# Quantised FFN: two places by turns for rows and scales, product clamped in bfloat16, first tile's second smoothing on VectorE, the gate's tanh later

## Chip, cores and metric

One core of one Trainium2 chip runs the whole program. The metric is device time in microseconds (us) of one execution; lower is better.

## What is computed

Two blocks of a gated cross-attention network, each an attention and a feed-forward part, on x of 8 x 256 rows of 1024 numbers. The diff touches only the last part, the quantised feed-forward network of the second block. For each row:

```
xs    = bf16(layernorm(x)) * inv_smooth          # once with inv_gate, once with inv_up
scale = max(max|xs| / 127, 1e-8)                 # one number per row
q     = clip(round(xs / scale), -127, 127)
gate  = (qg @ w_gate.T) * sg * s_wgate           # 1024 -> 512
up    = (qu @ w_up.T)   * su * s_wup
inter = bf16(clip(silu(gate) * up, -10, 10))
qi, si = quantise(inter * inv_inter)             # as above
out   = (qi @ w_down.T) * si * s_wdown           # 512 -> 1024
x     = x + tanh(g_ffn[1]) * out
```

## The kernel before

The parts before it (lag attention, routed experts, context attention) are not touched. `quantised_ffn` handles the 2048 rows as 16 tiles of 128 rows; a tile lies on the 128 partitions. Each engine has its own instruction list, written out by hand, and they meet through semaphores. `pipeline` calls an engine's `step` once for every tile number t from -3 to 17; within it, `on(2)` is the tile t + 2, `on(0)` the tile t, and so on, so that four stages of four tiles are worked on in one step. The steps 3 to 12 are a hardware loop (ten turns), the others are written out.

The stages of one tile, by engine:

- ACT normalises the rows to bfloat16 (`xf`), last in its step, for tile t + 3.
- POOL multiplies by the two smoothing rows (`xs_g`, `xs_u`), for tile t + 2.
- DVE takes the largest absolute value of each (`peak`), makes the scale (`scale_x`) and its reciprocal (`inv_x`).
- ACT rounds by adding a large constant (`xq_g`, `xq_u`), for tile t + 1; PE transposes; ACT subtracts the constant (`q`).
- PE multiplies by the gate and up weights into banks 4 and 5, for tile t; DVE scales them (`gated`, `up`), ACT takes silu, DVE multiplies (`hidden`) and clamps to bfloat16 (`hidden_b`), POOL smooths (`hs`), DVE makes `scale_h` and `inv_h`.
- ACT rounds (`hq`), PE transposes and multiplies by the down weights for tile t - 1; DVE scales (`y`) and POOL adds the residual (`final`) for tile t - 2; SP stores it.

DVE's order in a step is `y`, `gated`, `up`, product, clamp, two peaks, `scale_x`, `inv_x`, the peak of `hs`, `scale_h`, `inv_h`. POOL's is `xs_g`, `xs_u`, `final`, `hs`. ACT's is `xq_g`, `xq_u`, `hq`, silu, `q_h`, four times `q`, `xf`.

`xf`, `xs`, `inv_x` and `y` have one place each. POOL's `xs` of a tile therefore waits for ACT's reading of the tile before (semaphore `magic_x`). `ffn.rows` (shown as `ffn_row` in the trace) are the smoothing rows; `norm` makes mean and scale of the rows, and for the last batch (tiles 14 and 15) this is done within this part: `norm.variance` on DVE, `norm.on_pool` on POOL.

Of the kernel before, what the change touches and what calls it, by code (L numbers as in the profile page):

```python
# [1613 lines left out]
def quantised_ffn(nc, ffn, w_down_T, s_gate, s_up, s_down, inv_inter, gate, X, norm, out):  # L1614
# [4 lines left out]
    with ExitStack() as ctx:  # L1619
# [18 lines left out]
        plus_magic = sb("plus_magic", [P, 1])  # L1638
        xf = sb("xf", [P, D], BF16)
        xs = [sb("xs_g", [P, D]), sb("xs_u", [P, D])]  # L1640
        xq = [sb("xq_g", [P, D]), sb("xq_u", [P, D])]
        q = [sb("q_g", [P, KD, P], BF16), sb("q_u", [P, KD, P], BF16)]
        peak, inv_x = (sb(n, [P, 2]) for n in ("peak", "inv_x"))
        scale_x = sb("scale_x", [P, TILES, 2])
        gated, up = (sb(n, [P, HIDDEN]) for n in ("gated", "up"))
        hidden_b = sb("hidden_b", [P, HIDDEN], BF16)
        hs = sb("hs", [P, HIDDEN])
# [14 lines left out]
        def pipeline(eng, step):  # L1662

            def one(t):
                step(lambda off: t + off if not isinstance(t, int) or 0 <= t + off < TILES else None)
            for t in range(-3, 3):
                one(t)
            with eng.Fori(3, TILES - 3) as t:  # L1670
# [24 lines left out]
        def _(pool):  # L1695
# [5 lines left out]
                               pattern=[[-1, P]], channel_multiplier=1).then_inc(s["consts"], 1)  # L1701
            pool.dma_start(w_d[:].rearrange("p (k n) -> p k n", k=KH), w_down_T.rearrange("(k p) n -> p k n", p=P)).then_inc(s["w_d_in"], 16)
            norm.prepare(pool)
            for i in range(2):
                pool.wait_ge(ffn.rows_in[i], 16)

            def step(on):
                a, m, e = on(2), on(0), on(-2)
                if isinstance(a, int) and a == 2:
                    norm.on_pool(pool, B - 1, 0)  # L1710
                if a is not None:
                    for i, ready in enumerate(("xg_ready", "xu_ready")):
                        pool.wait_ge(s["xf_ready"], a + 1)

                        at_least(pool, s["magic_x"], 2 * (a - 1) + i + 1 if not (isinstance(a, int) and a == 0) else 0)
                        pool.tensor_tensor(xs[i][:], xf[:], smooth[i][:], ALU.mult).then_inc(s[ready], 1)  # L1716
                if e is not None:
                    pool.wait_ge(s["y_ready"], 2 * e + 2)
                    at_least(pool, s["stored"], 16 * e)
                    pool.tensor_tensor(final[:], y[:], tile_of(X, e), ALU.add).then_inc(s["added"], 1)  # L1720
                if m is not None:
                    if isinstance(m, int) and m == 0:
                        pool.wait_ge(vec_in[4], 16)
                    pool.wait_ge(s["hidden_b"], m + 1)
                    at_least(pool, s["magic_h"], m)
                    pool.tensor_tensor(hs[:], hidden_b[:], smooth_h[:], ALU.mult).then_inc(s["hs"], 1)  # L1726
# [3 lines left out]
        def _(act):  # L1730
            act.wait_ge(s["gate_in"], 16)
            act.activation(tg[:], tg[:], ACT.Tanh).then_inc(s["tg_done"], 1)
            act.wait_ge(s["consts"], 3)

            def step(on):
                a, f, m, d = on(3), on(1), on(0), on(-1)
                if f is not None:
                    for i in range(2):
                        act.wait_ge(s["scale_ready"], f + 1)
                        at_least(act, s[("turned_g", "turned_u")[i]], f)  # L1740
                        act.activation(xq[i][:], xs[i][:], ACT.Identity, scale=inv_x[:, i:i + 1], bias=plus_magic[:, 0:1]).then_inc(s["magic_x"], 1)  # L1741
                if d is not None:
# [17 lines left out]
                if a is not None:  # L1760
                    at_least(act, s["xg_ready"], a)
                    at_least(act, s["xu_ready"], a)
                    if not isinstance(a, int) or a >= TILES - 2:
                        act.wait_ge(norm.ready, 1)
                    act.activation(xf[:], tile_of(X, a), ACT.Identity,
                                   scale=norm.scale[:, bass.ds(a, 1)], bias=norm.shift[:, bass.ds(a, 1)]).then_inc(s["xf_ready"], 1)
            pipeline(act, step)

        @block.vector
        def _(dve):  # L1770
            norm.variance(dve, X, B - 1, 0)

            def step(on):
                a, m, e = on(2), on(0), on(-2)
                if isinstance(m, int) and m == 0:
                    dve.wait_ge(vec_in[2], 16)
                    dve.wait_ge(vec_in[3], 16)
# [5 lines left out]
                if e is not None:  # L1783
                    for i in range(2):
                        dve.wait_ge(s["down_pe"], 2 * e + i + 1)
                        at_least(dve, s["added"], e)
                        dve.scalar_tensor_tensor(out=y[:, i * 512:(i + 1) * 512], in0=bank[7 - i][:], scalar=scale_h[:, bass.ds(e, 1)],  # L1787
                                                 in1=scale_d[:, i * 512:(i + 1) * 512], op0=ALU.mult, op1=ALU.mult).then_inc(s["y_ready"], 1)
# [4 lines left out]
                if m is not None:  # L1793
# [4 lines left out]
                    dve.wait_ge(s["up"], m + 1)  # L1798
                    dve.tensor_tensor(bank[5][:], bank[4][:], up[:], ALU.mult).then_inc(s["hidden"], 1)  # L1799
                    dve.wait_ge(s["hidden"], m + 1)  # L1800
                    at_least(dve, s["hs"], m)
                    dve.tensor_scalar(hidden_b[:], bank[5][:], SWIGLU_LIMIT, -SWIGLU_LIMIT, ALU.min, ALU.max).then_inc(s["hidden_b"], 1)  # L1802
                if a is not None:
                    for i, ready in enumerate(("xg_ready", "xu_ready")):
                        dve.wait_ge(s[ready], a + 1)
                        dve.tensor_reduce(peak[:, i:i + 1], xs[i][:], AX_X, ALU.max, apply_absolute_value=True).then_inc(s["chain"], 1)  # L1806
                    dve.wait_ge(s["chain"], 3 * a + 2)
# [16 lines left out]
        def _(pe):  # L1824
            pe.wait_ge(s["consts"], 3)

            def step(on):
# [116 lines left out]
```

## Time and profile before

| | |
|---|---|
| median of 3 runs | 1379.06 us (1376.68 to 1380.38) |
| the profiled execution | 1376.35 us, its span 1374.6 us |
| the quantised part | from 1201.4 us of the span to its end |
| one turn of its loop | from 1283.25 to 1292.61 us, as an example |
| granted clock of PE, mean over the span | 0.974 of full speed |

The page counts busy time over the whole span, which has stages of quite different kinds. For a change in one stage the timeline of that stage is to be read, engine by engine: a row of it has the start, the length, the instruction, and in brackets how long the engine stood idle before it and what ended that. The length of an instruction can hold a wait that no semaphore shows.

### The profile page before, as it was taken

To read this page: it belongs to the slowest core of one execution; us is meant where nothing else is said; L and a number is where in the kernel's file an instruction comes from. 1 tells how busy PE (TensorE), PEld (TensorE's weight loads), DVE (VectorE), ACT (ScalarE), POOL (GpSimd) and SP (SyncE) were. 2 spreads that over 40 slices of the span, in tenths; PEclk is the share of its full clock that TensorE was granted. 3 is DMA by queue.
4 is the path that set the end of the run, shared out by engine and by line. 5 is a ranking of instruction groups with operands and counts; after the bars stand their busy time and mean duration, and the time that the engine had idled before them with its cause. 6 is when DMAs were issued, how large, how long until landed. Compare 5 with 4: busy or idle time off the path is not lost. (4 is left out here: it accounts for less than half of the span.)

```text
span 1374.6 us, 20874 instructions
## 1 busy us (share of the span) xinstructions
PE 1259.7 (92%) x6498; PEld 857.0 (62%) x6498; DVE 779.1 (57%) x2009; ACT 501.8 (37%) x875; POOL 579.4 (42%) x964
## 2 busy tenths in 40 slices
PE   4899999999977999999999998999999999858786
PEld 2354544545433955448887787888888898535443
DVE  3878888888774572005533333444454443368895
ACT  2544444444432600013322222232222322178884
POOL 5676867768653000003222221523212231168885
PEclk9999999999998999999999999999999999979999
DMA  5210211402001800416777874526334331121111
GB/s 198 89 66 31 92 61 45 184 15 88 35 0 47 324 1 7 144 59 243 256 250 249 275 260 158 191 85 134 107 110 123 94 103 50 62 69 46 61 61 77
DMA packets 52481, 156.38 MB, mean 114 GB/s; under 512 B 5952, under 2 KB 16192, under 8 KB 52288
## 3 DMA queue, kind: packets, MB, share of 16 engines
q1 hardware_dynamic: 39152, 113.60, 23.2%
q0 software_dynamic: 13264, 41.95, 10.7%
q8 instruction: 37, 0.61, 0.2%
q14 instruction: 28, 0.23, 0.1%
HBM read 113.06 MB, written 45.61 MB: 115 GB/s over the span
## 5 line engine op out<-in xcount | busy, mean ns | idle before, releaser
L1213 PEld LDWEIGHTS ex_bank<-ex_xT,ex_gu 128*112 128x112 f32 x1248 | 140.5, 177 | 24.9 <-issue 23.9
L1213 PE MATMUL ex_bank<-ex_xT,ex_gu 128*112 128x128 f32 x1248 | 143.6, 273 | 2.7 <-issue 1.8
L44 PE MATMUL xa_bank<-fT_high,M_hi 128*128 128x256 f32 x512 | 143.9, 281 | 0.0
L46 PE MATMUL xa_bank<-fT_high,M_lo 128*128 128x256 f32 x512 | 142.9, 279 | 0.0
L45 PE MATMUL xa_bank<-fT_low,M_hi 128*128 128x256 f32 x512 | 142.9, 279 | 0.0
L52 PE MATMUL la_bank<-la_osum,la_tab 128*128 128x512 f32 x256 | 120.6, 616 | 13.1 <-POOL la_osum L295 11.9
L295 POOL TENSOR_TENSOR la_osum<-la_oprod 128x512 f32<-128x512 f32 x64 | 80.2, 1273 | 96.1 <-DVE la_oprod L481 96.1
L1077 POOL TENSOR_TENSOR ex_small<-listed,ex_small 128x1 int32<-128x1 int32 x42 | 15.4, 368 | 225.0 <-DVE Wk L1155 224.9
L44 PEld LDWEIGHTS xa_bank<-fT_high,M_hi 128*128 128x128 f32 x512 | 96.5, 189 | 0.3
L46 PEld LDWEIGHTS xa_bank<-fT_high,M_lo 128*128 128x128 f32 x512 | 96.6, 189 | 0.0
L45 PEld LDWEIGHTS xa_bank<-fT_low,M_hi 128*128 128x128 f32 x512 | 96.3, 188 | 0.0
L52 PEld LDWEIGHTS la_bank<-la_osum,la_tab 128*128 128x128 f32 x256 | 47.7, 196 | 75.2 <-issue 48.3
L1433 DVE SCALAR_TENSOR_TENSOR X<-ffn_row,weights,X 128x1024 f32<-128x1024 f32 x30 | 38.6, 1285 | 92.3 <-DMA ffn_row<-produced,xa_small_u 91.8
L52 PE MATMUL la_bank<-la_v_raw,la_tab 128*128 128x512 f32 x128 | 64.4, 627 | 24.4 <-ACT la_v_spec L351 13.8
L52 PE MATMUL la_bank<-la_wT,la_tab 128*128 128x512 f32 x192 | 85.1, 593 | 1.2 <-ACT la_wT L378 1.2
L481 DVE TENSOR_TENSOR la_oprod<-la_bank,la_v_spec 128x512 f32<-128x512 f32 x128 | 79.7, 684 | 9.0 <-POOL la_osum L295 4.6
L1364 ACT ACTIVATE xa_G<-xa_bank,shift 128x256 f32<-128x256 f32 x64 | 30.4, 475 | 126.1 <-PE xa_bank L46 125.6
L1223 PE MATMUL ex_bank<-ex_dn,ex_hT 112*128 112x512 f32 x156 | 73.5, 593 | 0.4 <-DVE ex_hT L1166 0.4
L1155 DVE COPY Wk<-ex_xr 128x1024 f32 (+1 forms) x41 | 28.0, 684 | 71.5 <-PE ex_bank L700 71.5
L654 POOL TENSOR_TENSOR running_ln_small<-running_ln_mv,running_ln_small 128x2 f32<-128x2 f32 x32 | 6.3, 198 | 142.4 <-DVE running_ln_mv L683 141.1
L52 PEld LDWEIGHTS la_bank<-la_wT,la_tab 128*128 128x128 f32 x192 | 36.4, 190 | 46.9 <-issue 45.4
L700 PE MATMUL ex_bank<-Wq,Wk 128*128 128x512 f32 x144 | 62.1, 593 | 1.5 <-POOL ex_ident L1065 1.5
(281 smaller groups left out, 2807.0 us busy)
## 6 DMA issues: line engine op xcount, KB each, us to landing
produced<-Wk SPq DMA_DIRECT2D x39, 512.0 KB
ex_gu<-in_gate_up SPq DMA_DIRECT2D x16, 896.0 KB
X<-in_x SPq DMA_DIRECT2D x8, 1024.0 KB, 7.5
la_v_raw<-in_ctx SPq DMA_DIRECT2D x16, 512.0 KB, 4.0
produced<-la_zeros SPq DMA_DIRECT2D x16, 512.0 KB, 4.8
normal<-rt_xn SPq DMA_DIRECT2D x16, 512.0 KB, 5.4
fT<-in_ctx_T SPq DMA_DIRECT2D x8, 1024.0 KB, 5.4
xa_f<-in_ctx SPq DMA_DIRECT2D x8, 1024.0 KB, 4.9
```

Of the source, the lines that this page charges most:

```text
L44: pe.matmul(out, a[0], b[0], start=first, stop=False)
L45: pe.matmul(out, a[0], b[1], start=False, stop=False)
L46: return pe.matmul(out, a[1], b[0], start=False, stop=last)
L52: return pe.matmul(out, a, b, start=first, stop=last)
L295: pool.tensor_tensor(osum[:, i, :], oprod[:, a, :], oprod[:, a + 1, :], ALU.add if i % 2 == 0 else ALU.subtract).then_inc(s["osums"], 1)
L481: dve.tensor_tensor(oprod[:, 2 * (i % 2) + k, :], bank[bk][:], v_spectrum(u, vk), ALU.mult).then_inc(s["oprods"], 1)
L700: last = pe.matmul(out, W[1][:, k, (n // 2) * P:(n // 2 + 1) * P], W[0][:, k, (n % 2) * 512:(n % 2 + 1) * 512], start=(k == 0), stop=(k == ...
L1155: dve.tensor_copy(xs, xr[:, bass.ds(g % 2, 1), :].rearrange("p o d -> p (o d)")).then_inc(s["rows_held"], 1)
L1213: m = pe.matmul(bank[half][0:INTER, 0:P], gu[:, slot, at:at + INTER], xT[:, k, :], start=(k == 0), stop=(k == KD - 1))
L1223: m = pe.matmul(bank[4 + i][:], hT[:], dn[:, slot, i * 512:(i + 1) * 512], start=True, stop=True)
L1364: act.activation(G[:, m, :], bank[2 + m % 2][:, 0:L], ACT.Identity, bias=shift[:, m:m + 1]).then_inc(s["g_out"], 1)
L1433: dve.scalar_tensor_tensor(out=x, in0=landing(b, i), scalar=row_gate[:, bass.ds(n, 1)], in1=x, op0=ALU.mult, op1=ALU.add).then_inc(s["comb ...
```

## The change

`xf`, `xs_g`, `xs_u`, `inv_x` and `y` get two places, used by turns (`turn_of`, the tile number modulo 2); the waits for the buffers go back by one tile more. The product of silu and `up` is written to SBUF in bfloat16 (`product`) instead of to PSUM bank 5 in float32, and the clamp reads it there; PE's next `up` product waits for `up` having been read, no longer for the clamp. `xs_u` of tile 0 is made on DVE. The load of the down weights, `norm.prepare` and the last batch's scales on POOL move behind the smoothing of tile 1; the last batch's statistics on DVE move behind tile 0. ACT's tanh of the gate, with its wait for the gate's load, moves behind the second `xf`.

```diff
+        def turn_of(buffer, t):
+            return tile_of(buffer, t % 2)
...
@@ POOL
-            pool.dma_start(w_d[:].rearrange("p (k n) -> p k n", k=KH), w_down_T.rearrange("(k p) n -> p k n", p=P)).then_inc(s["w_d_in"], 16)
-            norm.prepare(pool)
...
                     for i, ready in enumerate(("xg_ready", "xu_ready")):
+                        if isinstance(a, int) and a == 0 and i == 1:
+                            continue
                         pool.wait_ge(s["xf_ready"], a + 1)
-                        at_least(pool, s["magic_x"], 2 * (a - 1) + i + 1 if not (isinstance(a, int) and a == 0) else 0)
-                        pool.tensor_tensor(xs[i][:], xf[:], smooth[i][:], ALU.mult).then_inc(s[ready], 1)
+                        at_least(pool, s["magic_x"], 2 * (a - 2) + i + 1)
+                        if isinstance(a, int) and a == 1 and i == 1:
+                            pool.wait_ge(s["xu_ready"], 1)
+                        pool.tensor_tensor(turn_of(xs[i], a), turn_of(xf, a), smooth[i][:], ALU.mult).then_inc(s[ready], 1)
+                if isinstance(a, int) and a == 1:
+                    pool.dma_start(w_d[:].rearrange("p (k n) -> p k n", k=KH), w_down_T.rearrange("(k p) n -> p k n", p=P)).then_inc(s["w_d_in"], 16)
+                    norm.prepare(pool)
+                    norm.on_pool(pool, B - 1, 0)
@@ ACT
-            act.wait_ge(s["gate_in"], 16)
-            act.activation(tg[:], tg[:], ACT.Tanh).then_inc(s["tg_done"], 1)
-            act.wait_ge(s["consts"], 3)
...
                 if a is not None:
-                    at_least(act, s["xg_ready"], a)
-                    at_least(act, s["xu_ready"], a)
+                    at_least(act, s["xg_ready"], a - 1)
+                    at_least(act, s["xu_ready"], a - 1)
...
+                if isinstance(a, int) and a == 1:
+                    act.wait_ge(s["gate_in"], 16)
+                    act.activation(tg[:], tg[:], ACT.Tanh).then_inc(s["tg_done"], 1)
+                    act.wait_ge(s["consts"], 3)
@@ DVE
-            norm.variance(dve, X, B - 1, 0)
+            dve.wait_ge(ffn.rows_in[1], 16)
+            dve.wait_ge(s["xf_ready"], 1)
+            dve.tensor_tensor(turn_of(xs[1], 0), turn_of(xf, 0), smooth[1][:], ALU.mult).then_inc(s["xu_ready"], 1)
...
-                        at_least(dve, s["added"], e)
+                        at_least(dve, s["added"], e - 1)
...
-                    dve.tensor_tensor(bank[5][:], bank[4][:], up[:], ALU.mult).then_inc(s["hidden"], 1)
+                    dve.tensor_tensor(product[:], bank[4][:], up[:], ALU.mult).then_inc(s["hidden"], 1)
...
-                    dve.tensor_scalar(hidden_b[:], bank[5][:], SWIGLU_LIMIT, -SWIGLU_LIMIT, ALU.min, ALU.max).then_inc(s["hidden_b"], 1)
+                    dve.tensor_scalar(hidden_b[:], product[:], SWIGLU_LIMIT, -SWIGLU_LIMIT, ALU.min, ALU.max).then_inc(s["hidden_b"], 1)
@@ PE
-                        at_least(pe, s[("hidden", "hidden_b")[i]], m)
+                        at_least(pe, s[("hidden", "up")[i]], m)
```

On DVE within the loop, the stretch from the product to the reciprocal of `inv_x` stands like this before; `REGISTER_ALU` and `ISA` rows are the computing of addresses and of waits:

```order
L1799 TENSOR_TENSOR qf_bank<-qf_bank,qf_up 128x512
L1802 TENSOR_SCALAR qf_hidden_b<-qf_bank 128x512
L1805 REGISTER_ALU
L1806 TENSOR_REDUCE qf_peak<-qf_xs_g 128x1
L1806 TENSOR_REDUCE qf_peak<-qf_xs_u 128x1
L1807 ISA
L1809 ISA
L1809 TENSOR_SCALAR qf_scale_x<-qf_peak 128x2
L1810 REGISTER_ALU
L1811 MEMSET qf_spare 128x1
L1812 RECIPROCAL qf_inv_x<-qf_scale_x 128x2
```

and like this in the changed kernel:

```order
L1812 TENSOR_TENSOR qf_product<-qf_bank,qf_up 128x512
L1815 TENSOR_SCALAR qf_hidden_b<-qf_product 128x512
L1818 REGISTER_ALU
L1819 ISA
L1819 TENSOR_REDUCE qf_peak<-qf_xs_g 128x1
L1819 REGISTER_ALU
L1819 TENSOR_REDUCE qf_peak<-qf_xs_u 128x1
L1820 ISA
L1822 ISA
L1822 TENSOR_SCALAR qf_scale_x<-qf_peak 128x2
L1823 REGISTER_ALU
```

The order of the work is the same; product and clamp have changed where they write and read, and a row or two of address computing has come in ahead of a peak and (below this piece) of the reciprocal and of both `y`.

At the start of the part, POOL's rows before are:

```order
L1700 AFFINE_SELECT qf_ident<-qf_ident 128x128
L1702 DMA qf_w_d<-in_w_down_T 128x4x1024
L643 MEMSET running_ln_small 128x2 x6
L644 MEMSET running_ln_small 128x2
L1716 TENSOR_TENSOR qf_xs_g<-qf_xf,ffn_row 128x1024
L1716 TENSOR_TENSOR qf_xs_u<-qf_xf,ffn_row 128x1024
L1716 TENSOR_TENSOR qf_xs_g<-qf_xf,ffn_row 128x1024
L1716 TENSOR_TENSOR qf_xs_u<-qf_xf,ffn_row 128x1024
```

and in the changed kernel:

```order
L1704 AFFINE_SELECT qf_ident<-qf_ident 128x128
L1720 TENSOR_TENSOR qf_xs_g<-qf_xf,ffn_row 128x1024 x2
L1720 TENSOR_TENSOR qf_xs_u<-qf_xf,ffn_row 128x1024
L1722 DMA qf_w_d<-in_w_down_T 128x4x1024
L643 MEMSET running_ln_small 128x2 x6
L644 MEMSET running_ln_small 128x2
```

One `xs_u` has left POOL (tile 0's, now DVE's first instruction of the part), and the load and the constants stand behind tile 1's smoothing.

ACT's first rows of the part before are:

```order
L1732 ACTIVATE qf_tg<-qf_tg 128x1
L1765 ACTIVATE qf_xf<-X,running_ln_shift,running_ln_scale 128x1024 x2
L1741 ACTIVATE qf_xq_g<-qf_xs_g,qf_plus_magic,qf_inv_x 128x1024
L1741 ACTIVATE qf_xq_u<-qf_xs_u,qf_plus_magic,qf_inv_x 128x1024
L1758 ACTIVATE qf_q_g<-qf_bank,qf_minus_magic 128x512 x2
```

and in the changed kernel:

```order
L1770 ACTIVATE qf_xf<-X,running_ln_shift,running_ln_scale 128x1024 x2
L1774 ACTIVATE qf_tg<-qf_tg 128x1
L1745 ACTIVATE qf_xq_g<-qf_xs_g,qf_plus_magic,qf_inv_x 128x1024
L1745 ACTIVATE qf_xq_u<-qf_xs_u,qf_plus_magic,qf_inv_x 128x1024
L1763 ACTIVATE qf_q_g<-qf_bank,qf_minus_magic 128x512 x2
```

The tanh, which waits for the load of the gate, has moved behind the `xf` of tiles 0 and 1.

## Rows read from the trace of the kernel before

**Rows 1.** page: span, busy time and its share, instructions
```profile
span 1374.6 us, 20874 instructions
...
PE 1259.7 (92%) x6498; PEld 857.0 (62%) x6498; DVE 779.1 (57%) x2009; ACT 501.8 (37%) x875; POOL 579.4 (42%) x964
```

**Rows 2.** busy time of each engine from 1250 to 1300 us
```profile
1250.00:1300.00 50.00, 42.03 (x245) 24.76 (x244) 44.27 (x79) 42.56 (x56) 42.62 (x23) 1.00 0.13 53
```

**Rows 3.** timeline of DVE, one step: start us, length us, instruction
```profile
1283.25 1.41 DVE L1787 SCALAR_TENSOR_TENSOR qf_y<-qf_bank,qf_scale_h,qf_scale_wd 128x512 f32<-128x512 f32 x2 [0.41 <-issue]
...
1286.08 0.70 DVE L1799 TENSOR_TENSOR qf_bank<-qf_bank,qf_up 128x512 f32<-128x512 f32 x1
1286.82 0.69 DVE L1802 TENSOR_SCALAR qf_hidden_b<-qf_bank 128x512 bf16<-128x512 f32 x1
1287.42 1.21 DVE L1806 TENSOR_REDUCE qf_peak<-qf_xs_g 128x1 f32<-128x1024 f32 x1
1288.55 1.21 DVE L1806 TENSOR_REDUCE qf_peak<-qf_xs_u 128x1 f32<-128x1024 f32 x1
1289.90 1.01 DVE L1809 TENSOR_SCALAR qf_scale_x<-qf_peak 128x2 f32 x1
...
1291.04 0.67 DVE L1815 TENSOR_REDUCE qf_peak_h<-qf_hs 128x1 f32<-128x512 f32 x1
...
1292.61 1.41 DVE L1787 SCALAR_TENSOR_TENSOR qf_y<-qf_bank,qf_scale_h,qf_scale_wd 128x512 f32<-128x512 f32 x2 [0.41 <-issue]
```

**Rows 4.** timeline of POOL, the same step
```profile
1283.19 2.15 POOL L1716 TENSOR_TENSOR qf_xs_g<-qf_xf,ffn_row 128x1024 f32<-128x1024 bf16 x1 [1.66 <-ACT qf_xq_g L1741]
...
1287.41 2.36 POOL L1720 TENSOR_TENSOR qf_final<-qf_y,X 128x1024 f32<-128x1024 f32 x1
1289.71 1.18 POOL L1726 TENSOR_TENSOR qf_hs<-qf_hidden_b,qf_smooth_h 128x512 f32<-128x512 bf16 x1
1292.55 2.15 POOL L1716 TENSOR_TENSOR qf_xs_g<-qf_xf,ffn_row 128x1024 f32<-128x1024 bf16 x1 [1.66 <-ACT qf_xq_g L1741]
```

**Rows 5.** timeline of ACT, the same step
```profile
1291.23 1.24 ACT L1741 ACTIVATE qf_xq_g<-qf_xs_g,qf_plus_magic,qf_inv_x 128x1024 f32<-128x1024 f32 x1 [1.04 <-DVE qf_inv_x L1812]
...
1298.30 1.25 ACT L1765 ACTIVATE qf_xf<-X,running_ln_shift,running_ln_scale 128x1024 bf16 x1
```

**Rows 6.** groups of DVE lines, 1180 to 1375: count, busy us, mean ns
```profile
L1809 DVE TENSOR_SCALAR qf_scale_x<-qf_peak 128x2 f32 x10 | 8.4, 838 | 1.5
...
L1781 DVE TENSOR_SCALAR qf_scale_wd<-qf_scale_wd,qf_tg 128x1024 f32<-128x1024 f32 x1 | 0.8, 755 | 0.0
```

**Rows 7.** timeline at 51 us, lag attention, DVE and POOL
```profile
51.28 1.26 POOL L270 TENSOR_TENSOR la_q_less<-la_q_n 128x512 f32<-128x512 f32 x1
51.66 1.16 DVE L435 SCALAR_TENSOR_TENSOR la_wt<-la_rest,la_wt 128x256 f32<-128x256 f32 x1 [0.18 <-ACT la_wt L367]
...
52.51 1.45 POOL L271 TENSOR_TENSOR la_q_n<-la_q_n 128x512 f32<-128x512 f32 x1
```

**Rows 8.** chain of waits at the stage start: start us, us, what
```profile
1201.40 2.48 DMA qf_tg<-in_g_ffn
...
1205.42 2.13 POOL qf_xs_g L1716
...
1211.14 0.17 DVE qf_inv_x L1812
...
1217.57 1.12 ACT qf_xf L1765
```

**Rows 9.** timeline of DVE: the scaling of tiles 0 and 11, and a free scale step
```profile
1236.48 1.41 DVE L1787 SCALAR_TENSOR_TENSOR qf_y<-qf_bank,qf_scale_h,qf_scale_wd 128x512 f32<-128x512 f32 x2
...
1262.69 0.17 DVE L1809 TENSOR_SCALAR qf_scale_x<-qf_peak 128x2 f32 x1
...
1339.06 1.41 DVE L1787 SCALAR_TENSOR_TENSOR qf_y<-qf_bank,qf_scale_h,qf_scale_wd 128x512 f32<-128x512 f32 x2
```

**Rows 10.** DMA issues from 1195 to 1250 us: KB, us to landing
```profile
qf_w_d<-in_w_down_T POOLq DMA_DIRECT2D x1, 1024.0 KB, 12.5
```

More of the change, by code:

```diff
@@ L1638, in quantised_ffn @@
         plus_magic = sb("plus_magic", [P, 1])
-        xf = sb("xf", [P, D], BF16)
-        xs = [sb("xs_g", [P, D]), sb("xs_u", [P, D])]
+        xf = sb("xf", [P, 2, D], BF16)
+        xs = [sb("xs_g", [P, 2, D]), sb("xs_u", [P, 2, D])]
         xq = [sb("xq_g", [P, D]), sb("xq_u", [P, D])]
         q = [sb("q_g", [P, KD, P], BF16), sb("q_u", [P, KD, P], BF16)]
-        peak, inv_x = (sb(n, [P, 2]) for n in ("peak", "inv_x"))
+        peak = sb("peak", [P, 2])
+        inv_x = sb("inv_x", [P, 2, 2])
         scale_x = sb("scale_x", [P, TILES, 2])
         gated, up = (sb(n, [P, HIDDEN]) for n in ("gated", "up"))
-        hidden_b = sb("hidden_b", [P, HIDDEN], BF16)
+        product, hidden_b = (sb(n, [P, HIDDEN], BF16) for n in ("product", "hidden_b"))
         hs = sb("hs", [P, HIDDEN])
@@ L1652, in quantised_ffn @@
         q_h = sb("q_h", [P, KH, P], BF16)
-        y = sb("y", [P, D])
+        y = sb("y", [P, 2, D])
         final = sb("final", [P, D])
@@ L1719, in step @@
                     at_least(pool, s["stored"], 16 * e)
-                    pool.tensor_tensor(final[:], y[:], tile_of(X, e), ALU.add).then_inc(s["added"], 1)
+                    pool.tensor_tensor(final[:], turn_of(y, e), tile_of(X, e), ALU.add).then_inc(s["added"], 1)
                 if m is not None:
@@ L1740, in step @@
                         at_least(act, s[("turned_g", "turned_u")[i]], f)
-                        act.activation(xq[i][:], xs[i][:], ACT.Identity, scale=inv_x[:, i:i + 1], bias=plus_magic[:, 0:1]).then_inc(s["magic_x"], 1)
+                        act.activation(xq[i][:], turn_of(xs[i], f), ACT.Identity, scale=turn_of(inv_x, f)[:, i:i + 1],
+                                       bias=plus_magic[:, 0:1]).then_inc(s["magic_x"], 1)
                 if d is not None:
@@ L1760, in step @@
                 if a is not None:
-                    at_least(act, s["xg_ready"], a)
-                    at_least(act, s["xu_ready"], a)
+                    at_least(act, s["xg_ready"], a - 1)
+                    at_least(act, s["xu_ready"], a - 1)
                     if not isinstance(a, int) or a >= TILES - 2:
                         act.wait_ge(norm.ready, 1)
-                    act.activation(xf[:], tile_of(X, a), ACT.Identity,
+                    act.activation(turn_of(xf, a), tile_of(X, a), ACT.Identity,
                                    scale=norm.scale[:, bass.ds(a, 1)], bias=norm.shift[:, bass.ds(a, 1)]).then_inc(s["xf_ready"], 1)
+                if isinstance(a, int) and a == 1:
+                    act.wait_ge(s["gate_in"], 16)
+                    act.activation(tg[:], tg[:], ACT.Tanh).then_inc(s["tg_done"], 1)
+                    act.wait_ge(s["consts"], 3)
             pipeline(act, step)
@@ L1770, in _ @@
         def _(dve):
-            norm.variance(dve, X, B - 1, 0)
+            dve.wait_ge(ffn.rows_in[1], 16)
+            dve.wait_ge(s["xf_ready"], 1)
+            dve.tensor_tensor(turn_of(xs[1], 0), turn_of(xf, 0), smooth[1][:], ALU.mult).then_inc(s["xu_ready"], 1)
             def step(on):
                 a, m, e = on(2), on(0), on(-2)
+                if isinstance(a, int) and a == 1:
+                    norm.variance(dve, X, B - 1, 0)
                 if isinstance(m, int) and m == 0:
@@ L1785, in step @@
                         dve.wait_ge(s["down_pe"], 2 * e + i + 1)
-                        at_least(dve, s["added"], e)
-                        dve.scalar_tensor_tensor(out=y[:, i * 512:(i + 1) * 512], in0=bank[7 - i][:], scalar=scale_h[:, bass.ds(e, 1)],
+                        at_least(dve, s["added"], e - 1)
+                        dve.scalar_tensor_tensor(out=turn_of(y, e)[:, i * 512:(i + 1) * 512], in0=bank[7 - i][:], scalar=scale_h[:, bass.ds(e, 1)],
                                                  in1=scale_d[:, i * 512:(i + 1) * 512], op0=ALU.mult, op1=ALU.mult).then_inc(s["y_ready"], 1)
@@ L1805, in step @@
                         dve.wait_ge(s[ready], a + 1)
-                        dve.tensor_reduce(peak[:, i:i + 1], xs[i][:], AX_X, ALU.max, apply_absolute_value=True).then_inc(s["chain"], 1)
+                        dve.tensor_reduce(peak[:, i:i + 1], turn_of(xs[i], a), AX_X, ALU.max, apply_absolute_value=True).then_inc(s["chain"], 1)
                     dve.wait_ge(s["chain"], 3 * a + 2)
@@ L1811, in step @@
                     dve.memset(spare[:], 0.0)
-                    dve.reciprocal(inv_x[:], scale_now).then_inc(s["scale_ready"], 1)
+                    dve.reciprocal(turn_of(inv_x, a), scale_now).then_inc(s["scale_ready"], 1)
                 if m is not None:
```

2 lines of the change are left out of this document (removed).

## Prediction

> **What bounds it now.** The page says that PE is busy 92% of the span [rows 1], but that is the sum over stages of which the diff touches only the last one, the quantised feed-forward part from 1201 us on. There the table of busy time by stretch is the first view to read: of 50 us DVE works 44.27, POOL 42.62, ACT 42.56 and PE 42.03 [rows 2]. No engine is full; four engines hand each other work in a ring, and the ring sets the time. So the timeline of one loop step comes next, and the reader is to lay three engines side by side.
>
> DVE starts to scale the output at 1283.25 and again at 1292.61 [rows 3]: a step is 9.36 us. POOL starts `xs_g` at 1283.19 and goes without a gap through `xs_u`, `final` and `hs`, the last one from 1289.71 for 1.18, that is until 1290.89. Then it stands for 1.66 us until ACT has read the old `xs_g` [rows 4]. ACT reads it at 1291.23 [rows 5], since it waits for the reciprocal, which waits for DVE's `scale_x`. This last one is the odd row: a `TENSOR_SCALAR` on 128x2 numbers that lasts 1.01 us, from 1289.90 to 1290.91 [rows 3]. Ten of them have a mean of 838 ns [rows 6]; one that met no POOL instruction took 0.17 [rows 9]. Its end, 1290.91, is the end of POOL's `hs`, 1290.89, on which it has no semaphore. So POOL's running instruction shuts this DVE instruction out. The same is seen at 51 us: a DVE instruction with two SBUF tensors starts at 51.66 and ends at 52.82, shortly after POOL's instruction that ends at 52.54, and POOL's next one, started at 52.51, takes 1.45 where its neighbour takes 1.26 [rows 7]. So DVE gets in at the boundary between two POOL instructions, and POOL pays for it a little.
>
> The ring is thus: `xs_g`, `xs_u`, `final`, `hs` (1290.89 − 1283.19 = 7.70), port free, `scale_x`, reciprocal, `xq_g`, next `xs_g` (1.66).
>
> **The change, part by part.** The sum is made in the profiled execution.
>
> *Two places for xf, xs, inv_x and y.* POOL no longer waits for ACT's reading of the tile before, but for the one two back: the 1.66 wait goes. What is late next is `xf`, which ACT still makes last in its step: from the end of `scale_x` (1290.91) to the end of `xf` (1298.30 + 1.25 = 1299.55) are 8.64 us [rows 3, 5]. The loop now computes which half of a buffer it wants: two register instructions or so more ahead of `y` and of the reciprocal. The row before them shows 0.41 of idle time for such instructions ahead of `y` [rows 3]; I put 0.16 for all on DVE (bounds 0 and 0.41).
>
> *Product in bfloat16 in SBUF.* The multiplication keeps its price (0.70, still one PSUM and one SBUF input). The clamp read PSUM and took 0.69, and 0.60 until the next started [rows 3]. Now source and result are in SBUF, as with `scale_x` and with the one f32 `TENSOR_SCALAR` of 1024 elements that took 0.755, while a reduction of as many takes 1.21 [rows 6, 3]. Its work lies between 0.17 (128x2, [rows 9]) and 0.60; I take 0.28, below half of 0.755 with its fixed part kept. The gain is 0.32 a tile. The price is that it now belongs to the kind that `scale_x` is, and must wait for POOL's running instruction: between 0 and 2.36 us (`final`, [rows 4]) per tile.
>
> The Trainium skill (SBUF — State Buffer, Who interferes with whom) says that `tensor_scalar` in a two-port mode and GpSimd exclude each other for a whole instruction; by it the clamp waits here, and the sum is the one below. If only the f32 form did, the sum would be that of the first rival.
>
> *One step, walked through.* DVE from the end of the clamp to the request of `scale_x`: 1289.90 − 1287.42 = 2.48. Its work 0.18. From its end to `y`: 1292.61 − 1290.91 = 1.70, with the registers 1.86. From `y` to the clamp's request: 1286.82 − 1283.25 = 3.57. Clamp 0.28. Sum without waits 8.37. POOL needs 1.25 for `hs` with its hand-over, 2.12 for each `xs`, 2.30 for `final`.
>
> Step A, the clamp ends at 0. `hs` runs to 1.25; `xf` comes only at 2.8 (see B), so the port is free at 2.48: `scale_x` ends at 2.66, `y` starts at 4.5, the clamp is asked for at 8.1. POOL meanwhile: `xs_g` 2.9 to 5.0, `xs_u` to 7.15, `final` to 9.5. The clamp waits about 1.3 and ends at 9.65.
> Step B. `xf` ends 8.64 after A's `scale_x`, at 11.3, which is 1.65 of B. `xs_g` runs 1.75 to 3.9, so `scale_x`, asked for at 2.48, waits until 3.75 and ends at 3.9; `y` starts at 5.8 and ends at 7.2, `final` runs 7.3 to 9.6, and the clamp, asked for at 9.35, ends at 9.75. The next `xf` ends at 3.9 + 8.64 = 12.5, which is 2.8 of A. The pattern closes on itself: 9.65 and 9.75, mean 9.7.
>
> So one wait of 1.66 is exchanged for one of about 1.3 on DVE itself per step. Before, tiles 0 to 11 took (1339.06 − 1236.48)/11 = 9.33 each [rows 9]. Eleven steps cost 11 × 0.37 = +4.1.
>
> *The start.* ACT's first `xf` waited for the gate's load, 1201.40 + 2.48 = 1203.88 [rows 8]; now it starts at about 1201.5 and ends at 1202.75. DVE does `xs_u` of tile 0 at once, about 1.22 (as a 1024 reduction, [rows 3]); it has two SBUF inputs, as the instruction at 51.66 has, so POOL's `xs_g` waits, and runs 1203.9 to 1206.0 instead of 1205.42 to 1207.55 [rows 8]. Two reductions end at 1208.4, but POOL goes straight on to tile 1 (no buffer holds it back), 1206.0 to 1210.2, so `scale_x` waits until then. The reciprocal comes at 1210.35 instead of 1211.14: of 2.4 us won 0.8 are left. ACT's third `xf` follows the transposes, 1217.57 − 1211.14 = 6.43 later as before: 1216.8. That is −0.8; the clamps of tiles 0 and 1, both ahead of the first `y`, give 0.32 each and find POOL idle: first `y` at 1235.0 instead of 1236.48 [rows 9], −1.5.
>
> *Moves that I cost at nothing.* The gate's tanh goes behind two `xf`, where ACT would wait for `scale_x`, and its user, the scaling of `scale_wd`, comes 30 us later. The load of `w_d` is issued some 8 us later, at 1210.2; 12.5 us to landing [rows 10] make 1223, and its first use is the matmul just ahead of the first `y`, past 1230. If it came later than that, the difference would be added once. The statistics of the last batch move behind tile 0 on DVE, about 2.9 us, where DVE waited for `xs_g`; they are needed for tiles 14 and 15 alone. `up` may overwrite its bank earlier; PE doesn't wait there now.
>
> *The end.* Tiles 12 to 15 have no `xs`; the clamp meets `final` once or twice: +0.8, an estimate (0 to 2.3).
>
> Sum: −1.5 + 4.1 + 0.8 = **+3.4**, so 1376.35 + 3.4 = 1379.8 for an execution like the profiled one. That one lies 2.7 below the median of the three runs, 1379.06; beside that median the same sum is 1382.5, and I give 1382. A measurement of this kernel tells 0.3%, 4.1 us, from no change, so this is no change that can be told, close to slower.
>
> **Rivals.** The mechanism above has 0.70 of the chance: 0.40 that it stays within 4.1 us of before, own range −1 to +4.1 (1378 to 1383 by the median), and 0.30 that it lands a little above, since a step over 9.77 decides it, and registers at 0.41 or a clamp of 0.45 bring the step to 9.85 and the sum to +5 or +6.
> 1. *The clamp takes no port*: it stays out of the two-port kind, or its bfloat16 form does. For it: no row shows a bfloat16 clamp that reads SBUF. Against it: `scale_x` is such an instruction in f32 and is shut out. A step is then 8.3, and 8.6 if it keeps its 0.60: 11 × (8.3 − 9.33) − 1.5 = −12.8, or 11 × (8.6 − 9.33) − 1.5 = −9.5. By the median 1366 to 1370. Chance 0.15.
> 2. *The waits fall kindly*: `final` is done each time the clamp is asked for, and `xs_g` starts late. A step is 8.4 to 9.1, the time −3 to −11 with start and end, 1368 to 1376. For it: the waits hang on 0.1 to 0.3 us, as that of `scale_x` does now (asked for at 1289.90, `hs` started at 1289.71). Against it: the two steps above bring each other about. Chance 0.08.
> 3. *Slower: at a boundary POOL's queued instruction gets in ahead of DVE's.* `scale_x` in step B then waits out `xs_u` too, 2.1 us in every second step: 5 × 2.1 = +10 on top, 1392. It decides once this happens in one step of ten. For it: POOL now always has an instruction queued there. Against it: the one such boundary in the rows, 52.54, went to DVE [rows 7]. Chance 0.07.
>
> **Numbers.** Faster 0.15 + 0.08 = 0.23, same 0.40, slower 0.30 + 0.07 = 0.37. The range reaches from the middle of rival 1 and 2, 1368, to 1389, which is a mean step of 10.3, and leaves out rival 3 and the far end of rival 1.
>
> **What would show it.** Clamp rows in the loop of 0.3 and of about 1.6 us by turns, with ends at the ends of POOL's `final`; `scale_x` of 0.18 and about 1.4 by turns; POOL's idle time ahead of `xs_g` released by `xf`, not by `xq_g`; steps of 9.7; the reciprocal of tile 0 near 1210.4, first `y` near 1235. Wrong would be: clamp rows all near 0.3 (rival 1), steps all alike (rival 2), or a `scale_x` longer than 1.6 (rival 3).

## The result, and the profile after

The changed kernel takes 1389.06 us (median of 4 runs, 1387.76 to 1391.05) against 1378.14 us before (4 runs, 1376.68 to 1380.38): 1.0079 times as long, 95% interval 1.0058 to 1.01. That is 10.9 us slower; the forecast was 1382 with a range to 1389. The same kernel timed a second time (below) came to 1.0061 [1.0043, 1.0079], 8.1 us slower.

The page of the changed kernel, whose lines answer to [rows 1]; its profiled execution took 1387.86 us:

```profile
span 1386.1 us, 20988 instructions
...
PE 1267.9 (91%) x6492; PEld 863.3 (62%) x6498; DVE 787.7 (57%) x2010; ACT 502.2 (36%) x875; POOL 578.6 (42%) x963
```

The shares hardly differ from those before; the page can't show this change. Busy time of each engine (count behind it) in one stretch can. First the changed kernel, 1250 to 1300 us as in [rows 2] and then 100 us of the loop:

```profile
1250.00:1300.00 50.00, 40.67 (x219) 25.58 (x220) 43.04 (x80) 40.66 (x52) 37.73 (x20) 0.93 0.13 53
1240.00:1340.00 100.00, 80.43 (x433) 49.63 (x433) 87.61 (x146) 77.59 (x100) 76.33 (x40) 0.93 0.13 53
```

and the same 100 us of the kernel before:

```profile
1240.00:1340.00 100.00, 82.66 (x480) 48.60 (x478) 89.60 (x164) 84.53 (x108) 82.66 (x44) 1.00 0.14 58
```

Every engine does less: DVE 146 instructions instead of 164. PE's granted clock differs too, 0.93 instead of 1.00.

The timeline of DVE in the changed kernel, one bad step (start, length, instruction), to be laid beside [rows 3]:

```profile
1299.84 1.41 DVE L1800 SCALAR_TENSOR_TENSOR qf_y<-qf_bank,qf_scale_h,qf_scale_wd 128x512 f32 x2 [0.52 <-issue]
...
1303.40 1.67 DVE L1815 TENSOR_SCALAR qf_hidden_b<-qf_product 128x512 bf16<-128x512 bf16 x1
...
1307.47 1.99 DVE L1822 TENSOR_SCALAR qf_scale_x<-qf_peak 128x2 f32 x1
...
1311.38 1.41 DVE L1800 SCALAR_TENSOR_TENSOR qf_y<-qf_bank,qf_scale_h,qf_scale_wd 128x512 f32 x2 [0.52 <-issue]
```

and POOL in that step, beside [rows 4]:

```profile
1302.57 2.35 POOL L1728 TENSOR_TENSOR qf_final<-qf_y,X 128x1024 f32 x1
1305.15 1.17 POOL L1734 TENSOR_TENSOR qf_hs<-qf_hidden_b,qf_smooth_h 128x512 f32<-128x512 bf16 x1 [0.23 <-DVE qf_hidden_b L1815]
1307.30 2.14 POOL L1720 TENSOR_TENSOR qf_xs_g<-qf_xf,ffn_row 128x1024 f32 x1 [0.98 <-ACT qf_xf L1770]
1309.40 2.14 POOL L1720 TENSOR_TENSOR qf_xs_u<-qf_xf,ffn_row 128x1024 f32 x1
1313.18 2.36 POOL L1728 TENSOR_TENSOR qf_final<-qf_y,X 128x1024 f32 x1 [1.64 <-DVE qf_y L1800]
```

The clamp, 0.69 before and always alike, lasts 1.67. It ends at 1305.07, and POOL's `final` at 1304.92. `scale_x` comes at 1307.47, 0.17 after `xs_g` has started, and ends with it: 1309.46 against 1309.44. Two waits lie in one step of 1311.38 − 1299.84 = 11.54 us. The brackets at the right of POOL's rows show what this does to POOL: its `hs` now waits for the clamp, 0.23, and the late `y` makes `final` wait, 1.64. POOL, which shuts DVE out, is made idle by it.

The clamp over the whole part, one tile's view (ns: least, median, most), which stood at 0.69 for all sixteen before:

```profile
L1815 DVE TENSOR_SCALAR qf_hidden_b<-qf_product x16: 293/748/2429, 1226.1 to 1370.9; 128x512 bf16<-128x512 bf16 x16
```

and both instructions in the groups of lines of 1240 to 1350 us (count, busy us, mean ns, idle before), where [rows 6] had 838 for `scale_x`:

```profile
L1815 DVE TENSOR_SCALAR qf_hidden_b<-qf_product 128x512 bf16<-128x512 bf16 x11 | 13.6, 1241 | 0.4
L1822 DVE TENSOR_SCALAR qf_scale_x<-qf_peak 128x2 f32 x10 | 8.8, 880 | 1.4
```

Then the account, in the two profiled executions, from the start of the part (the issue of the gate's load) on:

| stretch | before | after | difference | forecast |
|---|---|---|---|---|
| part's start to first `y` (1238.08) | 35.08 | 33.45 | −1.6 | −1.5 |
| first `y` to that of tile 11 (1351.85) | 102.58 | 113.77 | +11.2 | +4.1 |
| from there to the last `y` (1379.78) | 29.21 | 27.93 | −1.3 | +0.8 |
| sum | 166.87 | 175.15 | +8.3 | +3.4 |

The spans differ by 11.5. The other 3.2 lie ahead of the part, which starts at 1204.63 instead of 1201.40. No changed instruction stands there, and in the thirteen profiled executions of this study it starts anywhere from 1201.40 to 1206.25, in no order that follows the edits. So it is spread between executions, and what the traces show of the change itself is 8.3 us; in the profile of the second timing the part is 175.1 long, 8.2 more than before. The two timings give 10.9 and 8.1.

And the clock of 0.93? The timeline of PE in the changed kernel, behind the bad step (start, length of the group):

```profile
1307.47 1.89 PE L1851 MATMUL qf_bank<-ffn_w,qf_q_u 128*128 128x512 bf16 x8
...
1313.32 0.65 PE L1857 MATMUL qf_bank<-qf_ident,qf_hq 128*128 128x128 f32 x4 [3.96 <-ACT qf_hq L1751]
1313.81 1.27 PE L1864 MATMUL qf_bank<-qf_ident,qf_xq_g 128*128 128x128 f32 x8
1314.87 1.91 PE L1864 MATMUL qf_bank<-qf_ident,qf_xq_u 128*128 128x128 f32 x8
1316.57 2.55 PE L1870 MATMUL qf_bank<-qf_w_d,qf_q_h 128*128 128x512 bf16 x8
1318.96 1.89 PE L1851 MATMUL qf_bank<-ffn_w,qf_q_g 128*128 128x512 bf16 x8
```

and its busy table there, whose third number from the right is the granted clock:

```profile
1314.00:1316.00 2.00, 2.00 (x14) 2.00 (x13) 1.86 (x4) 1.66 (x4) 1.77 (x2) 0.62 0.00 0
1316.00:1319.00 3.00, 3.00 (x13) 1.52 (x12) 2.76 (x6) 2.56 (x4) 0.94 (x1) 0.68 0.43 175
1319.00:1322.00 3.00, 3.00 (x16) 1.34 (x15) 2.29 (x7) 3.00 (x4) 2.38 (x2) 1.00 0.00 0
```

PE stood still for 3.96 us; then for a few microseconds it is granted 0.62 to 0.68, a mean of both levels of its clock (1.2 and 2.4 GHz), and eight matmuls take 1.91 and 2.55 that take 1.04 and 1.89 a step earlier. In the loop of before its pause is 1.78 us and the clock stays at 1.00. In the changed kernel PE then works without a gap from 1313.32 to 1322.41, about 1.8 us late by the longer rows, and this reaches the other engines: ACT waits for the transposes (0.33 and 0.44 us from 1315 on), and DVE's `up` of 1322.72 waits 0.48 for its bank.

### The profile page after: what moved, and what is told of

Its sections match the earlier page's. It is cut to its first block and busy times, and to the rows that moved or that the text cites. A ratio compares the mean times of both kernels' runs of the same rounds, so it can differ in the third digit from the quotient of the medians.

```text
span 1386.1 us, 20988 instructions
## 1 busy us (share of the span) xinstructions
PE 1267.9 (91%) x6492; PEld 863.3 (62%) x6498; DVE 787.7 (57%) x2010; ACT 502.2 (36%) x875; POOL 578.6 (42%) x963
## 5 line engine op out<-in xcount | busy, mean ns | idle before, releaser
L1077 POOL TENSOR_TENSOR ex_small<-listed,ex_small 128x1 int32<-128x1 int32 x42 | 15.4, 368 | 225.6 <-DVE Wk L1155 225.5
L1180 DVE COPY Wk<-ex_bank 128x512 f32<-128x512 f32 x39 | 27.0, 692 | 65.3 <-ACT Wk L1133 65.3
```

## The experiments

"Changed" is the kernel after the change. Every ratio is against the kernel before, timed on the same chip; "part" is the length of the quantised part up to the last `y`, in the profiled execution, 166.9 before and 175.2 changed.

**1. The clamp back in PSUM.** If the clamp's place is the cause, this alone must win all back.

```diff
-dve.tensor_tensor(product[:], bank[4][:], up[:], ALU.mult)
+dve.tensor_tensor(bank[5][:], bank[4][:], up[:], ALU.mult)
...
-dve.tensor_scalar(hidden_b[:], product[:], SWIGLU_LIMIT, ...
+dve.tensor_scalar(hidden_b[:], bank[5][:], SWIGLU_LIMIT, ...
...
-at_least(pe, s[("hidden", "up")[i]], m)
+at_least(pe, s[("hidden", "hidden_b")[i]], m)
```

> The changed kernel with one part undone: product and clamp go through PSUM bank 5 in float32 as before, and PE waits for the clamp again. Theory (the clamp that reads and writes SBUF is shut out while POOL runs): clamp rows all 0.69 us and none longer, mean step from the first to the twelfth y near 8.7 us instead of 10.3, time 6 us under the kernel before (about 17 under the changed one). Rival 1 (the two places and their address computing make the step long, the clamp is innocent): step stays at 10 or more, time within 3 us of the changed kernel.

1374.29 us, 0.9973 [0.9958, 0.9989]; the part 162.1. Its groups of lines on DVE, 1240 to 1350 us:

```profile
L1815 DVE TENSOR_SCALAR qf_hidden_b<-qf_bank 128x512 bf16<-128x512 f32 x12 | 8.3, 692 | 0.4
L1822 DVE TENSOR_SCALAR qf_scale_x<-qf_peak 128x2 f32 x10 | 1.8, 182 | 1.5
```

and its busy time, 1240 to 1340:

```profile
1240.00:1340.00 100.00, 88.37 (x506) 51.81 (x509) 87.10 (x176) 91.05 (x116) 86.50 (x45) 1.00 0.14 58
```

No clamp waits any more, and within the loop `scale_x` has stopped waiting too (182 ns); the steps of the loop are 8.74, the clock is 1.00. 13 us of the part hang on where the clamp reads, though in PSUM its own work is more than twice as long (0.69 against 0.29). The kernel is 4 us faster than before, where 6 were expected. The first `y` comes 36.05 us after the part's start, 2.6 later than in the changed kernel: `scale_x` of tile 2 is asked for at 1230.56, just after POOL has begun `xs_g` at 1230.35, and lasts 1.96 instead of 0.17.

**2. The clamp alone in SBUF**, in the kernel before, with one place for each buffer (the edit above, reversed).

> The kernel before with the clamp part alone: product in bfloat16 in SBUF, PE waits for up. One place each as before. Theory: the clamp is asked for while POOL runs xs_u, waits about 0.5 us and saves 0.3 of its own, and scale_x behind it is shut out by hs until the same moment as before, so the step stays at 9.4 and the time within 2 us of before. Rival (the clamp wait costs whatever stands around it): step at 10 or more, time 7 or more above before.

1380.08 us, 1.0003 [0.9991, 1.0016]: no difference. Clamps are 0.79 and `scale_x` 0.96 in steps of 9.4. Each clamp meets only the end of `xs_u` (1290.96 + 0.80 = 1291.76, `xs_u` until 1291.60), so its wait is 0.5, what it saves is 0.4, and `scale_x` waits for `hs` as before. So the clamp's place costs nothing here and 13 us in the changed kernel: neither edit alone is slow (the two places alone are experiment 7), the two together are.

**3. `scale_x` in two halves** of one column each, in the changed kernel.

```diff
-dve.tensor_scalar(scale_now, peak[:], 1.0 / QMAX, 1e-8, ALU.mult, ALU.max)
+dve.tensor_scalar(scale_now[:, 0:1], peak[:, 0:1], 1.0 / QMAX, 1e-8, ALU.mult, ALU.max)
+dve.tensor_scalar(scale_now[:, 1:2], peak[:, 1:2], 1.0 / QMAX, 1e-8, ALU.mult, ALU.max)
```

> The changed kernel with scale_x made by two instructions of 128x1 in place of one of 128x2. Theory (only the two-port form is shut out, and scale_h, of 128x1, never shows a wait): both halves about 0.15 us without a wait; the clamp still waits; step near 9.2 to 9.5, time 8 us under the changed kernel. Rival (every DVE instruction of this kind is shut out by a running POOL instruction): the halves wait as scale_x did, time that of the changed kernel.

1377.92 us, 0.9997 [0.9984, 1.001]: the loss is gone by the medians (9 to 11 us), and 6.3 of it in the part (168.8), though the clamps wait as they did (17.6 us in sum instead of 15.4). Of the 6.3, 1.5 stand ahead of the first `y`, where `scale_x` of tile 0 no longer waits. The mean step is 9.64 instead of 10.34, with 9.2 to 9.5 expected. The timeline of DVE in this kernel:

```profile
1290.29 0.15 DVE L1822 TENSOR_SCALAR qf_scale_x<-qf_peak 128x1 f32 x1
1290.42 0.15 DVE L1823 TENSOR_SCALAR qf_scale_x<-qf_peak 128x1 f32 x1
```

and of POOL, whose `xs_g` runs over both halves:

```profile
1289.60 2.13 POOL L1720 TENSOR_TENSOR qf_xs_g<-qf_xf,ffn_row 128x1024 f32 x1 [0.47 <-ACT qf_xf L1770]
```

The one-column form isn't shut out: 32 such rows, all 0.14 to 0.16. So with one of the two waits gone most of the loss is gone.

**4. Both: clamp in PSUM, `scale_x` in halves.** Edits 1 and 3 together.

> The changed kernel with both: clamp through PSUM as before, and scale_x by halves of 128x1. Theory: no DVE row of the loop has a wait that no semaphore shows; step near 8.6, set by DVE's own work and by ACT; time 10 us under before. Rival (ACT's late xf bounds the step, not the port): step at 9.3 or more.

1372.0 us, 0.9952 [0.9937, 0.9968], the part 159.6. Neither of the two is shut out, and a step is still 8.86, where 8.6 was expected, and the kernel is 6.3 us under before, where 10 were: what remains is DVE's own work, with the clamp's 0.6, a second half of `scale_x` and address computing in it. In the loop the halves cost 0.12 a step more than experiment 1; what they win stands at the start, where the first `y` comes after 32.8 us instead of 36.05.

**5. The loop written out**, in the changed kernel: tile numbers are constants then, with nothing to compute.

```diff
-            for t in range(-3, 3):
-                one(t)
-            with eng.Fori(3, TILES - 3) as t:
-                one(t)
-            for t in range(TILES - 3, TILES + 2):
+            for t in range(-3, TILES + 2):
                 one(t)
```

> The changed kernel with the ten loop turns written out, so that the places taken by turns are fixed addresses and no register is computed. Theory (the address computing is the second thing that I priced too low; it stands behind waits on DVE and POOL, 0.68 us from inv_h to y against about 0.1 written out): step about 0.4 us shorter but the port waits stay, time 3 to 5 us under the changed kernel, still 5 above before. Rival (the address computing is hidden): time of the changed kernel within 2 us.

1385.16 us, 1.0041 [1.0023, 1.0058]: 2 to 4 us better than changed by the medians, though the intervals touch or overlap. The profiled execution is the slowest of the ten (1388.32, the fastest 1378.33). In it the steps are 12.1 to 12.7 and 7.55 by turns up to the tenth, with clamps of 2.1 to 2.4 and 0.45, `scale_x` of 1.3 and 0.17, some 1.9 us of waiting for PE in each long step, and again a clock of 0.93. Both waits fall into the same step here too. In this execution the time taken out of DVE's work is for the greater part given back as waiting.

**6. The product in float32**, in SBUF as in the changed kernel: is it the type or the place?

```diff
-        product, hidden_b = (sb(n, [P, HIDDEN], BF16) for n in ("product", "hidden_b"))
+        hidden_b = sb("hidden_b", [P, HIDDEN], BF16)
+        product = sb("product", [P, HIDDEN])
```

> The changed kernel with the product in SBUF in float32 instead of bfloat16; the clamp still writes bfloat16. Theory (it is the place of source and result, SBUF, that lets a running POOL instruction shut the clamp out, not the 16-bit form): waits as in the changed kernel, shortest clamp row 0.4 to 0.5 us instead of 0.29, time within 3 us of the changed kernel. Rival (only the 16-bit form is shut out): no clamp row over 0.7, time 5 us under before.

1388.3 us, 1.0075 [1.0054, 1.0097]: as the changed kernel. Its tile's view (ns: least, median, most):

```profile
L1816 DVE TENSOR_SCALAR qf_hidden_b<-qf_product x16: 426/883/2136, 1224.8 to 1370.2; 128x512 bf16<-128x512 f32 x16
```

The clamp by itself takes 0.43 instead of 0.29, and all sixteen wait 9.8 us in sum, against 10.7 for the bfloat16 ones. It is the place, not the type.

**7. Two places alone**: the start of before, the clamp in PSUM.

> The kernel before with only the two places by turns: clamp through PSUM, and the start of the part as before (tanh first, both smoothings of tile 0 on POOL, the load ahead of them). Beside the run with the clamp alone undone it prices the new start. Theory: step 8.74 as there, first y 35 us after the part begins; time 2 to 3 us under before. Rival (the gain of that run came from the start): time within 1 us of before.

1375.86 us, 0.9976 [0.9964, 0.9989]; steps of 8.74, the part 163.6. Against experiment 1, whose start is the changed one, 1.5 us more, all of it ahead of the first `y`: 37.5 against 36.05. The forecast had put 0.8 on the start's edits (the rest of its 1.5 was for two clamps); the times (1374.29 and 1375.86) can't tell this apart alone. The first `y` had been expected after 35 us, as before, and came 2.5 later: `scale_x` of tiles 0 and 2 lasts 0.83 and 1.96 where it lasted 0.17 and 0.17 before. So the two places alone bring waits for POOL at the start, and win by their shorter steps.

**8. Experiment 1, written out.**

> The changed kernel with the clamp through PSUM as before and the loop written out. Theory: neither port waits nor address computing; step 8.1 to 8.3, set by ACT's 8.1 of work; time 8 to 10 us under before, the fastest so far. Rival (writing out costs as much in instruction loading as the registers do): time as with the clamp undone alone, 4 under before.

1369.56 us, 0.9944 [0.9924, 0.9964]; steps of 8.14 instead of 8.74. So the hardware loop, with its computed addresses, wait values and branch, costs 0.6 us a step; the three are not told apart. On DVE it is more: `scale_x`, expected without a wait, takes 0.51 each, as DVE now comes to it before `hs` is done, and that wait of 0.34 fills a part of what was won.

**9. Everything: clamp in PSUM, halves, written out.**

> All three together: clamp through PSUM, scale_x by halves of 128x1, loop written out, with the two places and the new start of the changed kernel. Theory: the 0.35 us that scale_x still waits in each step of the run without the halves goes, and so do the 1.8 and 1.95 us of tiles 0 and 2; first y 33 us after the part begins, step 7.9 to 8.0, set by DVE's own work; time 3 to 4 us under that run, 1366. Rival (ACT, which there stands idle for 0.5 us a step, is the bound): time within 1.5 us of that run.

1365.19 us (5 runs), 0.9901 [0.9884, 0.9918]; the part 153.2. It is the fastest of the study, 14 us below before. Its 100 us:

```profile
1240.00:1340.00 100.00, 92.02 (x532) 55.34 (x543) 94.40 (x197) 92.61 (x122) 91.45 (x48) 1.00 0.16 64
```

Four engines are above 91%; steps are 7.83 to 8.48, mean 8.10, where 7.9 to 8.0 was expected, and the first `y` comes after 34.4 us, where 33 was.

**10. The changed kernel again**, to see whether its pattern of waits is chance.

> The changed kernel once more, on the same chip as the other kernels of this call, so that the ratio rests on more runs. Theory: 1.007 to 1.009 of before; waits of the clamp and of scale_x together 20 us or more as in its first profile. Rival (its first profile showed an unlucky phase of the waits): a ratio under 1.003.

1387.31 us, 1.0061 [1.0043, 1.0079]. Steps of 12.96, 8.83, 9.93, 11.52, 8.80 against 12.96, 8.82, 9.92, 11.53, 8.79 in the first profile: the pattern is the kernel's own and repeats to a few hundredths there. The waits come to 20.7 us in sum, as expected; the ratio lies a little under the 1.007 expected and well over the rival's 1.003.

**11. `xf` earlier**: in the changed kernel ACT makes `xf` right behind `xq_u` instead of last in its step.

```diff
                         act.activation(xq[i][:], turn_of(xs[i], f), ACT.Identity, ...
+                if a is not None:
+                    ...
+                    act.activation(turn_of(xf, a), tile_of(X, a), ACT.Identity, ...
...
-                if a is not None:
-                    ...
-                    act.activation(turn_of(xf, a), tile_of(X, a), ACT.Identity, ...
```

> The changed kernel with ACT making xf right behind xq_u instead of last in its step, so that POOL starts xs_g straight after hs. Nothing else moves. Theory (what a port wait costs depends on where POOL's instructions lie when DVE asks): scale_x always meets xs_g and waits about 0.8 to 1.0, the clamp always meets final or a gap; all steps alike, 9.5 to 9.8, time 3 to 7 us under the changed kernel. Rival (only the kind of the instruction counts, not the phase): steps of 10.1 to 10.3, time as the changed kernel.

1383.93 us, 1.0041 [1.0027, 1.0056], 3.4 better than changed by the medians, though the intervals overlap. Its groups of lines, 1240 to 1350:

```profile
L1822 DVE TENSOR_SCALAR qf_scale_x<-qf_peak 128x2 f32 x10 | 8.9, 887 | 1.5
...
L1815 DVE TENSOR_SCALAR qf_hidden_b<-qf_product 128x512 bf16<-128x512 bf16 x11 | 3.2, 293 | 0.4
```

The same instructions on both engines, only in another phase: no clamp of the loop waits (293 ns each), `scale_x` waits 0.72 in each turn, and the steps of the loop are nearly alike, 9.74 to 9.87 but for the first turn's 10.08. They don't get to 8.7, because ACT's silu now comes later and in most steps DVE's product waits for it:

```profile
1283.11 0.69 DVE L1812 TENSOR_TENSOR qf_product<-qf_bank,qf_up 128x512 bf16<-128x512 f32 x1 [0.73 <-ACT qf_bank L1761]
```

POOL waits for `y` and for the clamp. The view of waits (line waited for: us, times, longest) has it for POOL, 1240 to 1340:

```profile
POOL qf_final L1728 <- DVE qf_y L1800: 16.5, 10, 2.1
POOL qf_hs L1734 <- DVE qf_hidden_b L1815: 4.6, 10, 0.7
```

## Why the forecast was off

**Right: the mechanism.** The clamp is shut out by POOL's running instruction. All its long rows end where POOL's end, 0.15 after; by itself it takes 0.29, forecast 0.28. The Trainium skill (SBUF — State Buffer, Who interferes with whom) has it that a `tensor_scalar` in a two-port mode and a GpSimd instruction shut each other out for a whole instruction, and names `tensor_scalar` as one of the operations that can enter such a mode when its operands allow. The traces agree for a clamp from SBUF to SBUF (0.29 to 2.43 us), and for PSUM to SBUF it never happened (0.69, sixteen of sixteen, in all six kernels here that have it so). Rival 1 falls with it; experiment 6 shows the same for a product in float32.

**Right: the start.** The reciprocal of tile 0 came at 1213.48 in a part that began 3.23 later, that is 1210.25 on the clock of before; forecast 1210.35. `scale_x` of tile 0 lasted 1.80, until POOL's `xs_u` had ended, as the forecast had POOL go straight on. First `y` −1.6, forecast −1.5. What was costed at nothing shows no price in it.

**Right: POOL's wait.** For `xs_g` it was 17.3 us in 100 before, released by `xq_g`; now:

```profile
POOL qf_xs_g L1720 <- ACT qf_xf L1770: 16.7, 9, 3.9
POOL qf_final L1728 <- DVE qf_y L1800: 6.2, 4, 1.6
POOL qf_hs L1734 <- DVE qf_hidden_b L1815: 1.8, 8, 0.2
```

The releaser is the one named, `xf`. But the wait "goes" in name only: it is 16.7 now, and two more stand beside it, 24.7 in sum.

**Wrong: the walk through one step, and with it the term of eleven steps, +4.1, which measured +11.2.** The prediction said: "The pattern closes on itself: 9.65 and 9.75, mean 9.7." A step had one wait of 1.3, either the clamp's or `scale_x`'s. The chip shows steps of 8.79, 9.74 and 11.54 by turns, and toward the end 8.79 and 11.8 or 11.1; the first is 12.96, the mean 10.34. Both waits are long in five of the eleven steps. What the walk left out, for the eleven steps:

- Waits for POOL. Eleven clamps took 13.66 us, of which 11 × 0.29 is work, and eleven `scale_x` 10.46, of which 11 × 0.17 is work: 10.5 + 8.6 = 19.1 us of waiting, where the walk had 11 × 1.3 = 14.3. So +4.8.
- DVE waits for PE: 3.3 us in six places. The walk had none. The first two, 0.33 and 0.98, stand right behind the first `y`, ahead of any long step; in the base of 9.33 is one of 0.97 there. The other four, 2.0 in sum, come two steps behind a long one, such as 0.47 ahead of `up` at 1292.64: a step of 11.5 leaves PE idle for 4 us, and its matmuls are slower after that.

8.37 (the forecast's work of a step) + 19.1 / 11 + 3.3 / 11 = 10.41, and the measured step is 10.34. So the work was sized rightly within 0.1, and the waits not.

**The constant in the walk that failed is the 8.64 us from the end of `scale_x` to the end of the next `xf`** ("`xf` ends 8.64 after A's `scale_x`"). That distance is 8.63 or 8.64 in nine of ten steps of the kernel before. In the loop of the changed kernel it is never that short: 8.97 to 10.35 in ten steps, mean 9.63. One of the 8.97 is from the `scale_x` that ends at 1297.92 to this row's end, 1306.89:

```profile
1305.64 1.25 ACT L1770 ACTIVATE qf_xf<-X,running_ln_shift,running_ln_scale  x1
```

In the longest, ACT waits 0.94 and 0.43 us for PE's transposes (1285.65 and 1287.35), which are the slow ones behind a long step. And `xs_g` begins 0.41 after `xf`'s end (1306.89 to 1307.30), where the walk had 0.1. So POOL starts `xs_g` at least 0.6 later than forecast, by a time that changes from step to step; in the bad step shown above it starts just ahead of the request for `scale_x`, which then waits for all of it (1.99 instead of 1.3). Walked again by the same rules with 8.97 and 0.41 in place of 8.64 and 0.1, step A comes to about 10.2, B stays at 9.75, and the eleven steps cost +7.3: an estimate, not a run. The rest would be the steps in which `xf` is later still, and PE.

The runs bear this out in part. Experiment 1 removes both waits of the loop and experiment 3 that of `scale_x`, and most of the loss goes. In experiment 11, where ACT makes `xf` early, only `scale_x` waits, in nearly the same way in each step. That its step of 9.77 is near the 9.7 of the walk is chance: it is made of a wait of 0.72 for POOL and one of 0.73 for silu. The 0.41 alone doesn't decide: written out, where `xs_g` starts 0.07 after `xf`'s end (1288.98 to 1289.05), the waits meet as well (experiment 5). No run keeps PE's clock up with `xf` where it is, so how much of the pattern is due to each stays open.

**Wrong in size: the tail.** +0.8 forecast, −1.3 measured: the last three clamps took 0.46, 0.38 and 0.29 instead of 0.69 each, since they met POOL only at the end of an instruction or not at all. The gain stands in the step behind tile 11's `y`, 7.56 instead of 8.96, where the clamp gives 0.23 and DVE no longer waits 0.92 for POOL's `hs` (before, ahead of the row at 1347.03).

**Rival 3 was not seen.** At each boundary DVE got in: the clamp of 1294.22 ended at 1294.56, when POOL's `xs_u` ended at 1294.41 and `final` had been queued; `final`, begun at 1294.36, took 2.42 instead of 2.35. Five `scale_x` got in ahead of a queued `xs_u` in the same way. A `scale_x` of 1.99 is longer than 1.6, which was to be the sign of rival 3; but it is one instruction waited for from its start, and the sign was badly chosen.

The range's end, 1389, was worked out as "a mean step of 10.3", and 10.34 came. The chance of 0.30 for "a little above" was laid on registers and on the clamp's own time, not on the waits, and it is the waits that the excess came from.

## What to carry to other kernels

Before a DVE instruction is made faster by moving its input from PSUM to SBUF, look at POOL: where POOL is busy four fifths of a step, as here, the instruction gains 0.4 us and may wait up to 2.1, and the measured choice was the slow, undisturbed form (13 us better; with one place for each buffer it made no difference). A wait that depends on phase can't be priced by one hand-walked cycle with a distance taken from the kernel before (8.64 here, which became 8.97 to 10.35): cost it from zero to the whole of the other engine's instruction, let two such waits fall into the same step, and let the engine left idle by it (PE here) come back slower and hold up the next. Where an instruction of few numbers is shut out, splitting it to one column freed it here, and writing out a tight loop, with no computed addresses and no branch, was worth 0.6 us a step.

## What the runs showed of the hardware

- A `TENSOR_SCALAR` on 128x2 numbers in SBUF is shut out by a running POOL instruction (0.17 to 1.99 us in the changed kernel), the same on 128x1 is not (0.14 to 0.16 us, 96 rows in three kernels).
- A shut-out `scale_x` ends 0.02 us after POOL's instruction, a shut-out clamp 0.15 after it; a `final` begun meanwhile took 2.42 instead of 2.35.
- Behind 3.96 us without work PE was granted 0.62 of its clock from 1314 to 1316 and 0.68 from 1316 to 1319; behind the 1.78 us of the loop of before it kept 1.00.
- A hardware loop of 8.74 us a turn takes 8.14 written out; what is gone with it are the computing of addresses and of waits' values and the branch. In the profile it shows only as gaps, such as the 0.52 us ahead of each `y` of the changed kernel.
